# Row maxima from half the partitions: three leading products, two heads side by side on TensorE

## The reference, cut to what matters

```
q = Wq target + bq ; k = Wk source + bk ; v = Wv source + bv     # 8 batches, 16 heads of 16, 512 x 512
dot = einsum('bhdt,bhds->bhts', q, k) / sqrt(16)
mask = target_mask[..., None] * source_mask[..., None, :]
dot = mask * dot - (1 - mask) * 1e6
amap = softmax(dot, axis=-1) * mask
out = einsum('bhts,bhds->bhdt', amap, v)
```

## Time and profile before

| | |
|---|---|
| median of three runs | 1266.95 us |
| profiled execution: time, span in the profile | 1269.88 us, 1268.1 us |
| mean granted TensorE clock over the span | 0.941 |
| attention, from the first score to the last `pv` | 163.2 to 544.2 us |
| DVE reductions of the maxima (L802) | 512, 319.9 us busy |
| PE matmuls of the maxima (L718) | 512, first at 132.2 us |
| exponentials on ACT (L677) | 256, 250.7 us busy |

### The profile page before, as it was taken

How to read it: one execution, slowest core, us unless ns; L and a number is a source line. 1 busy time by engine, 2 the same in 40 slices (tenths; PEclk the granted TensorE clock), 3 DMA queues, 4 the chain that set the end, 5 groups by cost and what they waited for, 6 DMA issues and landing times. The chain is left out here.

```text
span 1268.1 us, 13982 instructions
## 1 busy us (share of the span) xinstructions
PE 1107.0 (87%) x4802; PEld 448.8 (35%) x4802; DVE 1026.4 (81%) x1568; ACT 673.8 (53%) x787; POOL 515.3 (41%) x403
## 2 busy tenths in 40 slices
PE   3977799999999999869999976999999998179586
PEld 2534122222222222124444433444444444034232
DVE  4778888888988988278999964887888878777898
ACT  1655168878878878946566652110000000686896
POOL 1756213345345335520011014878888883000021
PEclk9989589999999999999999997999999998599889
DMA  8799934455455443123111101121211110000011
GB/s 317 234 300 353 312 101 129 126 158 158 127 154 160 129 144 117 50 88 141 36 51 34 51 17 49 56 63 54 67 54 62 64 53 17 1 1 1 9 59 66
DMA packets 69319, 131.84 MB, mean 104 GB/s; under 512 B 18048, under 2 KB 35840, under 8 KB 65664
## 3 DMA queue, kind: packets, MB, share of 16 engines
q1 hardware_dynamic: 69248, 130.95, 32.4%
HBM read 106.53 MB, written 22.02 MB: 101 GB/s over the span
## 5 line engine op out<-in xcount | busy, mean ns | idle before, releaser
L802 DVE TENSOR_REDUCE mneg<-ps_m 128x1 f32<-128x512 f32 x512 | 319.9, 683 | 46.9 <-PE ps_m L718 46.6
L1362 PE MATMUL ps_y<-kv,toeplitz_sb 128*128 128x512 f32 x640 | 279.2, 595 | 8.8 <-POOL kv L1274 8.8
L677 ACT ACTIVATE probs<-ps_s 128x1024 f32<-128x1024 f32 x256 | 250.7, 1022 | 44.6 <-PE ps_s L741 44.5
L718 PE MATMUL ps_m<-k_stack,q_stack 112*128 112x512 bf16 x512 | 185.6, 404 | 10.3 <-DMA k_stack<-mask_k 9.2
L1362 PEld LDWEIGHTS ps_y<-kv,toeplitz_sb 128*128 128x128 f32 x640 | 120.9, 191 | 154.9 <-issue 154.9
L741 PE MATMUL ps_s<-q_stack,k_stack 112*128 112x512 bf16 x512 | 153.1, 382 | 13.8 <-ACT probs L677 13.5
L751 PE MATMUL ps_o<-probs,v_all 128*17 128x512 f32 x1024 | 135.9, 604 | 0.0
L1274 POOL TENSOR_TENSOR kv<-vT,ctxT_sb 128x2048 f32<-128x2048 f32 x32 | 118.8, 3713 | 39.0 <-PE ps_y L1362 32.0
L980 PE MATMUL ps_g<-w,xT_f 128*128 128x512 bf16 x512 | 120.7, 385 | 10.0 <-DVE h_f L1146 6.5
L1327 ACT ACTIVATE w_anchor<-w_f 128x512 f32<-128x512 f32 x32 | 20.1, 628 | 180.6 <-DMA w_f<-in_w 180.6
L1428 DVE TENSOR_TENSOR z<-ps_y,ctxT_sb 128x1024 f32<-128x1024 f32 x64 | 77.9, 1218 | 46.8 <-PE ps_y L1362 46.8
(11 more groups left out here) (159 smaller groups left out, 1627.6 us busy)
## 6 DMA issues: line engine op xcount, KB each, us to landing
w_sweep<-in_w SPq DMA_DIRECT2D x8, 1536.0 KB, 10.1
q_stack<-q_parts SPq DMA_DIRECT2D x96, 128.0 KB, 4.7
k_stack<-k_parts SPq DMA_DIRECT2D x96, 128.0 KB, 4.5
w_sweep<-in_w SPq DMA_DIRECT2D x16, 768.0 KB, 5.5
w_sweep<-in_w SPq DMA_DIRECT2D x16, 512.0 KB, 3.6
toeplitz_sb<-in_toeplitz SPq DMA_DIRECT2D x32, 256.0 KB, 2.6
w_f<-in_w SPq DMA_DIRECT2D x32, 256.0 KB, 2.9
k_parts<-qk_part SPq DMA_DIRECT2D x24, 256.0 KB, 6.4
```

The source lines that it names most:

```text
L677: nc.scalar.activation(pr[:, k % 2, 2 * slot:2 * slot + 2, :], S[:, 2 * slot:2 * slot + 2, :], ACT.Exp).then_inc(exp_done, 1)
L718: nc.tensor.matmul(M[:, bank(j), :], Q[slot][0:ROWS, hd, tc * P:(tc + 1) * P], K[slot][0:ROWS, hd, :], start=True, stop=True).then_inc(max ...
L802: nc.vector.tensor_reduce(mneg[:, h, tile % LT, tile // LT:tile // LT + 1], M[:, bank(j), :], AX.X, ALU.max, negate=True).then_inc(max_red, 1)
L1362: mm = nc.tensor.matmul(Y[:, q % 3, l2, :], T[:, g % 2, (lt - m) * P:(lt - m + 1) * P], kv[:, g % 2, m, :], start=(m == 0), stop=(m == lt))
```

## The change

- A stack now has two sides of 64 partitions. For head x below 4, side 0 (partitions 0 to 63) holds the three leading products and the mask rows, side 1 the other three products, with rows of constants (Q 0, K 1) in the place of the mask. For heads 4 to 7 the sides are exchanged. A row is 64 times the side, plus 4d, plus the product.
- A maximum tile multiplies only its head's leading side: 64 rows. `place` takes the tiles in turn from head x on side 0 and head x+4 on side 1.
- The scores take all 128 partitions, with all six products as before.
- m0 and m1 stand together between the two pairs of scores, where one stood between them and one behind the second.
- Q and K of a slot are now one tile, and the parts in DRAM one tensor. A unit's load is 12 DMAs of 128 KB (L77), each with two planes for four heads, and 4 mask DMAs of 64 KB (L82); for the first two batches 4 more of 64 KB for the constants (L85).
- The row of maxima goes to the stack in two DMAs (L547), to the side without the mask.

```diff
+LEAD = 3
+STEP = LEAD + 1
+SIDE = STEP * HD
+QUAD = UH // 2
+MAX_ROW = STEP * BLOCKS + LEAD
 def load_unit(core, sp, b, h):
+    planes = core.parts.rearrange("s b j c l -> (s b j) c l")
     for blk in range(BLOCKS):
-        for dst, src, part in ((core.Q, core.q_parts, Q_PART[blk]), (core.K, core.k_parts, K_PART[blk])):
-            s = src[b, part, h * P:(h + 1) * P, :]
-            sp.dma_start(dst[slot][blk:ROWS:STEP], s.rearrange("(d h) l -> d h l", d=HD))\
+        first, second = 3 * b + Q_PART[blk], 3 * (B + b) + K_PART[blk]
+        both = planes[first:second + 1:second - first, h * P:(h + 1) * P, :]\
+            .rearrange("s (d a x) l -> d a s (x l)", d=HD, a=2)
+        for a in range(2):
+            row = SIDE * (a if blk < LEAD else 1 - a) + blk % LEAD
+            sp.dma_start(core.QK[slot][row:SIDE * (row // SIDE + 1):STEP, :, QUAD * a:QUAD * (a + 1)]
+                         .rearrange("d s x l -> d s (x l)"), both[:, a]).then_inc(core.qk_loaded[slot], 16)
+    for a in range(2):
+        for dst, src in ((core.Q, core.mask_q), (core.K, core.mask_k)):
...
+            if b < 2:
...
+    def place(tile):
+        return tile % 2, QUAD * (tile % 2) + tile // (2 * LT), tile // 2 % LT
...
-            sp.dma_start(Q[slot][MAX_ROW:MAX_ROW + STEP + 1:STEP], mrow[:]).then_inc(m_placed[h], 16)
+            for a in range(2):
+                row = SIDE * (1 - a) + MAX_ROW
+                sp.dma_start(Q[slot][row:row + STEP + 1:STEP, QUAD * a:QUAD * (a + 1), :], mrow[UH * a:UH * (a + 1)])\
+                    .then_inc(m_placed[h], 16)
...
-        nc.tensor.matmul(M[:, bank(j), :], Q[slot][0:ROWS, hd, tc * P:(tc + 1) * P],
-                         K[slot][0:ROWS, hd, :],
+        rows = slice(SIDE * a, SIDE * (a + 1))
+        nc.tensor.matmul(M[:, bank(j), :], Q[slot][rows, hd, tc * P:(tc + 1) * P], K[slot][rows, hd, :],
...
                     scores(u, slot4, k, 0, start)
-                    maxima(ts[0:1])
+                    maxima(ts[0:2])
                     scores(u, slot4, k, 1, start)
-                    maxima(ts[1:2])
```

More of the change, by code:

```diff
@@ L28 @@
 BLOCKS = len(Q_PART)
[L29 to L32, removed]
+LEAD = 3
[3 more added lines that the diff above has]
+MAX_ROW = STEP * BLOCKS + LEAD
+SLOT_LOADS = 16 * (2 * BLOCKS + 4)
+SLOT_CONSTS = 16 * 4
 def batch_loads(b, par):
@@ L40, in slot_loads @@
 def slot_loads(b, par):
-    return (2 * BLOCKS + 2) * (8 * (b - par) + 16)
+    return SLOT_LOADS * ((b - par) // 2 + 1) + SLOT_CONSTS
 class Core:
@@ L66, in load_unit @@
     slot = 2 * (b % 2) + h
+    planes = core.parts.rearrange("s b j c l -> (s b j) c l")
     for blk in range(BLOCKS):
-        for dst, src, part in ((core.Q, core.q_parts, Q_PART[blk]), (core.K, core.k_parts, K_PART[blk])):
-            s = src[b, part, h * P:(h + 1) * P, :]
-            sp.dma_start(dst[slot][blk:ROWS:STEP], s.rearrange("(d h) l -> d h l", d=HD))\
[L71 to L74, removed]
+        first, second = 3 * b + Q_PART[blk], 3 * (B + b) + K_PART[blk]
[7 more added lines that the diff above has]
+        for dst, src in ((core.Q, core.mask_q), (core.K, core.mask_k)):
+            heads = dst[slot][:, QUAD * a:QUAD * (a + 1), :]
+            sp.dma_start(heads[SIDE * a + LEAD:SIDE * (a + 1):STEP],
+                         src[:, b].unsqueeze(1).to_broadcast([HD, QUAD, L])).then_inc(core.qk_loaded[slot], 16)
+            if b < 2:
+                sp.dma_start(heads[SIDE * (1 - a) + LEAD:SIDE * (2 - a):STEP],
+                             src[BLOCKS:BLOCKS + 1, 0].unsqueeze(1).to_broadcast([HD, QUAD, L]))\
+                    .then_inc(core.qk_loaded[slot], 16)
 def row_stats(core, t):
@@ L184, in store_parts @@
             sp.wait_ge(p3_ready, nth(b, s))
-            dst = (core.q_parts, core.k_parts)[s]
             for j in range(3):
-                sp.dma_start(dst[b, j].rearrange("(ct p) l -> p ct l", p=P), part[:, b % 2, s, j])\
+                sp.dma_start(core.parts[s, b, j].rearrange("(ct p) l -> p ct l", p=P), part[:, b % 2, s, j])\
                     .then_inc(qk_stored[b % 2], 16)
@@ L499, in phase_attention @@
     TURN_SLOT = EACH * (TURN_STEP + 1)
-    LOADS = 16 * (2 * BLOCKS + 2)
+    LOADS = SLOT_LOADS + SLOT_CONSTS
     def tiles(k, more, more2):
@@ L649, in rows_of_max @@
             if not same(v, 0):
-                act.wait_ge(m_placed[1 - h], 16 * before)
+                act.wait_ge(m_placed[1 - h], 32 * before)
             nc.scalar.activation(mrow[:], RT[0:2 * UH, 0:L], ACT.Copy).then_inc(mrow_ready, 1)
@@ L708, in max_tile @@
     def max_tile(pe, v, slot, tile, j):
-        hd, tc = tile // LT, tile % LT
+        a, hd, tc = place(tile)
         n = TILES * v + tile
@@ L740, in scores @@
                 hd = 2 * g + k // LT
-                mm = nc.tensor.matmul(S[:, g, :], K[slot4][0:ROWS, hd, (k % LT) * P:(k % LT + 1) * P],
-                                      Q[slot4][0:ROWS, hd, :], start=True, stop=True)
+                mm = nc.tensor.matmul(S[:, g, :], K[slot4][:, hd, (k % LT) * P:(k % LT + 1) * P],
+                                      Q[slot4][:, hd, :], start=True, stop=True)
             mm.then_inc(scores_done, 1)
@@ L767, in batch @@
                 slot4 = 2 * par + h
-                pe.wait_ge(m_placed[h], 16 * (b + 1))
+                pe.wait_ge(m_placed[h], 32 * (b + 1))
                 for k in range(STEPS):
@@ L801, in reduce_tile @@
         dve.wait_ge(max_mm, TILES * v + tile + 1)
-        nc.vector.tensor_reduce(mneg[:, h, tile % LT, tile // LT:tile // LT + 1], M[:, bank(j), :],
+        a, hd, tc = place(tile)
+        nc.vector.tensor_reduce(mneg[:, h, tc, hd:hd + 1], M[:, bank(j), :],
                                 AX.X, ALU.max, negate=True).then_inc(max_red, 1)
@@ L809, in split_max @@
             dve.wait_ge(m_turned, v - 1)
-        nc.vector.tensor_copy(mm16[:, h, :, 0:UH], mneg[:, h]).then_inc(m_parts, 1)
+        parts = mm16[:, h].rearrange("p t (a r x) -> p t a r x", a=2, r=2)
+        m = mneg[:, h].rearrange("p t (a x) -> p t a x", a=2)
+        nc.vector.tensor_copy(parts[:, :, :, 0], m).then_inc(m_parts, 1)
         dve.wait_ge(m_parts, v + 1)
-        nc.vector.tensor_tensor(mm16[:, h, :, UH:2 * UH], mneg[:, h], mm16[:, h, :, 0:UH], ALU.subtract)\
+        nc.vector.tensor_tensor(parts[:, :, :, 1], m, parts[:, :, :, 0], ALU.subtract)\
             .then_inc(m_split, 1)
@@ L1774, in build @@
     core.nc = nc
-    core.q_parts = nc.dram_tensor("q_parts", (B, 3, C, L), BF16, kind="Internal").ap()
-    core.k_parts = nc.dram_tensor("k_parts", (B, 3, C, L), BF16, kind="Internal").ap()
+    core.parts = nc.dram_tensor("qk_parts", (2, B, 3, C, L), BF16, kind="Internal").ap()
     core.v_rows = nc.dram_tensor("v_rows", (B, P, LT * HEADS * (HD + 1)), F32, kind="Internal").ap()
@@ L1805, in build @@
         KB = 1024
-        q0, k0, q1, k1 = overlay(nc, "low", 0, *((n, [P, UH, L], BF16) for n in (
-            "q_stack0", "k_stack0", "q_stack1", "k_stack1")))
+        qk0, qk1 = overlay(nc, "low", 0, *((n, [P, 2, UH, L], BF16) for n in ("qk_stack0", "qk_stack1")))
         core.proj = overlay(
@@ L1819, in build @@
                      rw_tmp)
-        q2, k2, q3, k3, *core.att = overlay(
-            nc, "att", 32 * KB, ("q_stack2", [P, UH, L], BF16),
-            ("k_stack2", [P, UH, L], BF16), ("q_stack3", [P, UH, L], BF16), ("k_stack3", [P, UH, L], BF16),
+        qk2, qk3, *core.att = overlay(
+            nc, "att", 32 * KB, ("qk_stack2", [P, 2, UH, L], BF16), ("qk_stack3", [P, 2, UH, L], BF16),
             ("probs", [P, 2, 4, L], F32), ("w_sweep2", [P, 2, 3, L], F32), ("inv_all", [P, 2, L], F32),
@@ L1826, in build @@
         core.w3, = overlay(nc, "w3", 124 * KB + KB // 2, ("w3", [P, 3, 4, FF], BF16))
-        core.Q, core.K = [q0, q1, q2, q3], [k0, k1, k2, k3]
+        core.QK = [qk0, qk1, qk2, qk3]
+        core.Q, core.K = [x[:, 0] for x in core.QK], [x[:, 1] for x in core.QK]
         core.w8 = core.w3[:, 0:2]
```

## The result

The changed kernel takes 1292.51 us (median of four runs, 1290.87 to 1293.80) against 1267.45 of before in the same series: ratio 1.0192, 95% interval 1.018 to 1.0204. Slower, as forecast (1286.0, range 1271 to 1298); the loss was 25.1 us where 19 were forecast. The profiled executions differ by less: 1291.67 against 1269.88, or 21.8 us.

What follows compares the result with a forecast made beforehand. PE bounds attention now; after the change m1's wait for its bank binds. Steps add 12.1 us and the later start 7 to 1269.9, giving 1289.0, or 1286.0 for the median 2.9 lower; range 1271 to 1298.

Steps and rivals of the forecast that it cites:

- Bound of the ordinary step: Six ordinary steps per unit: m1 waits for m2's bank, which DVE must reduce first; 2.99 us instead of 2.82.
- the chain: In the ordinary step: m2 to m1's release 1.17, then 0.31, 0.22, 0.31 and 0.98, giving 2.99 us.
- The rival with free row changes: On PE, layout changes by rows between scores and maxima cost nothing; 1276.6 us, chance 19%.
- the rival without overlap: On PE, the two 64-row halves do not run together; step 3.09 us, run 1295.5 us, chance 12%.
- the fourth rival: Not slower: results from 64 rows reach DVE sooner, passage shorter by 0.1 us, row changes free; 1267 us, chance 4%.
- The waiting step: The step from pv where the second scores wait for ACT: m1 hides in the wait, 3.215 us against 3.44.
- the one with transposes: The step where transposes wait for a reduction: 3.585 us against 3.555, or -0.07 with free row changes.
- The rival of the absorbed start: On SP, small DMAs are cheap and the start is absorbed, adding 1 us; 1280 us, chance 8%.
- which swallows 2.05: On SP, free time from 132.81 until 134.86 absorbs 2.05 of the 3.84 us that slot 0's six added DMAs cost.
- the fifth rival: The clock falls to 0.50 in attention because PE streams less in a longer step; above 1450 us, chance 2%.
- The range's ends: Whole run, 1271 to 1298 us: the ends come from the bounds, +2.6 + 1.4 and +21.5 + 9.5.

Runs made afterwards that it cites:

- shorter reductions: Reductions over 256 of the 512 columns, against the changed kernel with all else kept; 1263.72 us, one run, ordinary step 2.75 us.
- the order alone on the kernel before: m0 and m1 together between the score pairs, on 112 rows with loads as before, against the kernel before; 1274.55 us, ratio 1.0046.
- all rows: Maxima over all 128 rows instead of 64-row halves, against the changed kernel, with its order, loads and DMAs; 1283.79 us, one run.
- the placement first: First placement of the maxima on SP ahead of slot 2's load instead of behind it, against the changed kernel; 1287.87 us, ratio 1.0165.

## Why the prediction was right, step by step

- **Bound of the ordinary step.** Forecast 2.99, measured 3.01. Every term of the chain stood: m1 at the bank's release, 0.31 behind m0, then 0.32, 0.23, 0.31 and 0.98. The missing 0.02 are the second matmul after a change of layout (0.23, not 0.215) and the change itself (0.315 to 0.32, not 0.31). The shorter reductions and the order alone on the kernel before show the mechanism from both sides.
- **Row changes are not free.** Taken at 0.095, measured 0.10 (2.91 to 3.01 between all rows and row halves). The rival with free row changes, 19%, is out. The Trainium skill says in "TensorEngine Tiling (Array Packing)", Key Properties, that a change of the tiling mode drains TensorE. The traces agree in that a change by rows costs time, as one by columns does.
- **Halves run together.** Two in 0.39 us, the length of one; the rival without overlap, 12%, is out. Its price of 1295.5 came within 3 us of the result by accident, nearer than the forecast's 1286.0 with its 6.5.
- **A shorter way to DVE.** From m2's start to its reduction it is 0.42 (329.72 to 330.14) where 0.43 was taken, so 64 rows shorten nothing that counts; the fourth rival is out.
- **The waiting step and the one with transposes.** 3.215 and 3.585 forecast, 3.22 and 3.61 measured.
- **SP.** 0.64 per small DMA, the placement at 166.9, first scores near 170: measured 0.64 from one issue to the next, 166.86 and 169.55. The rival of the absorbed start is out. But that 166.9 was met is luck. The step "which swallows 2.05" failed: from the end of slot 0's load to the start of slot 1's SP took 137.01 - 125.79 = 11.22 before and 139.05 - 127.84 = 11.21 after, so the gap took nothing in. What made up for it is that SP began slot 0's load 2.35 us earlier in this execution than in the one of before (114.37 against 116.72). The change does not explain that: the load begins at 113.29 to 116.72 in the three traces with the loads of before and at 112.11 to 116.31 in the eight with the changed ones. Counted from the start of slot 0's load, the placement comes 52.49 - 40.66 = 11.8 us later and the first scores 55.18 - 46.52 = 8.7 later, where 9.5 and 7 were forecast. In the other traces with the order of SP unchanged the first scores come 46.3 and 47.8 us after it with the loads of before, and 54.2 to 54.4 with the changed ones.
- **The clock and the fifth rival.** The rival is out: the granted clock is 1.00 from 184 to 560 us. But the start holds a term that I had put at nothing: I took everything behind the first score as shifted, no more. It cost 1.5 us on top of the shift: 0.8 to the first `pv`, and 1.55 in unit 0, where 0.85 was due. These windows of the changed kernel (busy us by engine, granted clock, DMA share, GB/s) show why:

```profile
163.00:170.00 7.00, 2.43 (x6) 0.43 (x5) 3.12 (x6) 0.00 (x0) 0.00 (x0) 0.50 0.58 157
170.00:177.00 7.00, 6.57 (x22) 0.87 (x20) 3.86 (x6) 5.60 (x6) 0.00 (x0) 0.52 0.92 297
177.00:184.00 7.00, 7.00 (x41) 1.50 (x37) 5.41 (x9) 5.86 (x7) 1.23 (x2) 1.00 0.37 102
```

The clock is at 0.50 for the first 7 us of scores; before, the mean of 163 to 170 is 0.83, so it rose near 165.4, two microseconds after the first score:

```profile
163.00:170.00 7.00, 6.29 (x26) 1.81 (x26) 5.67 (x10) 5.58 (x6) 0.00 (x0) 0.83 0.96 262
```

Ahead of the first score PE of the changed kernel waited 4.57 us for the placement; in the kernel before it had tiles to multiply up to the first score. That wait alone does not explain the late rise. With the placement first PE does not wait for it, and is busy for 12.5 us of the 13 from 160 to 173, yet the clock is 0.50 all that time and rises about 8 us after the first score (165.45):

```profile
160.00:173.00 13.00, 12.53 (x32) 1.91 (x31) 10.51 (x18) 5.71 (x6) 0.00 (x0) 0.50 0.52 145
```

It rose 2 to 5 us after the first score in the three traces with the loads of before, and 4 to 11 us after it in the eight with the changed ones. In the one with all rows it had been up from 160 to 167 us and fell while PE waited. What sets the moment stays open.

- **The sum.** 19.1 forecast, 21.8 between the profiled executions: 2.2 more in units 1 to 13 (1.02 each for 0.85), 1.5 behind the first score, 0.2 in the last units, against 0.7 less for the first score itself and 0.6 at the end. Between the medians it is 25.1. Of the further 3.3, 2.35 are the later start of slot 0's load in the profiled execution of before; with it the two traces differ by 24.1, as an estimate, and 1 us is left that no trace locates. So the forecast was short by 6 us: 2.2 by the steps of units 1 to 13, 1.7 by the first score, 1.5 behind it, about 1 that is not located, and the rest small. The range's ends take +1.4 and +9.5 for the start, where the bounds worked out before them were +1 and +10.5; that moves the ends by 1 us at most and decides nothing.

## What to carry to other kernels

Packing two matmuls into one slot saves nothing if the second needs a buffer that its consumer frees later: work out the release time of each buffer on the way (here 0.43 + 0.74 us) before counting slots, and put the pair where both buffers are already free. Count the changes of array layout in the order, and group instructions of one layout. A small DMA cost its issuer as much here as one of twice its size (0.59 us of SP for 64 and for 128 KB), so look at what stands behind the added ones in the queue; putting the one urgent transfer ahead of a bulk load gave 4.6 us. And before two traces are subtracted, look whether they started alike: a start that lay 2.35 us apart hid a step of this prediction that had failed.

## What the runs showed that I had not expected

The second matmul behind a change of layout starts 0.23 us after the first, not 0.22. And moving one tile pair by a single place, with the same instructions, is worth 1.75 us in a unit of 24.90, more than the row halves themselves.
